# Cross-attention pair on one core: pair loop written out, row of maxima ahead of the loads of K and V, and eight slots in four batches with a second VectorE sum in the second attention

## The reference

```python
def layer0(Q, K, V):                      # 8 heads of 16; Q = x, K = V = ctx
    Qh, Kh, Vh = heads(Q @ W_q), heads(K @ W_k), heads(V @ W_v)
    attn = softmax(Qh @ Kh.T / sqrt(16))
    X = Q + merge(attn @ Vh) @ W_o
    return relu(X @ w1.T + b1) @ w2.T + b2 + X

def layer1(q_x, kv_x):                    # 16 heads of 32; q_x = layer0's result, kv_x = ctx
    q  = heads(layernorm(q_x) @ Wq.T)
    k, v = heads(layernorm(kv_x) @ Wkv.T)
    attn = softmax(q @ k.T / sqrt(32))
    x = q_x + merge(attn @ v) @ Wo.T + bo
    return x + silu(x @ W1.T + b1) @ W2.T + b2
```

## Time and profile before

| | |
|---|---|
| time, median of 3 runs (lowest, highest) | 5593.9 us (5593.8, 5606.19) |
| the profiled execution: its time, its span | 5599.11 us, 5597.3 us |
| granted TensorE clock, mean | 0.973 |
| TensorE (PE) busy | 5326.1 us, 95% |
| VectorE (DVE) | 4013.6 us, 72% |
| ScalarE (ACT) | 3170.5 us, 57% |
| GpSimd (POOL) | 2330.6 us, 42% |
| DMA, mean over the span | 58 GB/s |

### The profile page before, as it was taken

The page is one execution under the profiler, slowest core; times in us unless marked ns, Lnnn a source line. Parts: engine busy times, 40 slices in busy tenths (PEclk is TensorE's granted clock), DMA queues, the critical chain, the costliest instruction groups (busy, mean ns, idle before and its releaser), DMA issues. The chain is left out here.

```text
span 5597.3 us, 103454 instructions
## 1 busy us (share of the span) xinstructions
PE 5326.1 (95%) x28684; PEld 3349.3 (60%) x28684; DVE 4013.6 (72%) x6947; ACT 3170.5 (57%) x5792; POOL 2330.6 (42%) x1156
## 2 busy tenths in 40 slices
PE   8989999999799799999999999999999996999999
PEld 6744444444377456555565556555565563777777
DVE  6688888899577688887887878888788885332331
ACT  4257777788533366666666666666666664322222
POOL 0000000000000388888888878878888886000000
PEclk9989999999899799999999999999999998999999
DMA  7521111111343311111111111111111112322220
GB/s 214 128 47 38 36 36 39 36 38 32 98 134 108 102 41 28 40 40 41 39 29 41 40 41 34 36 39 40 41 29 40 41 28 63 111 93 68 86 88 23
DMA packets 329713, 325.64 MB, mean 58 GB/s; under 512 B 185744, under 2 KB 193808, under 8 KB 327184
## 3 DMA queue, kind: packets, MB, share of 16 engines
q1 hardware_dynamic: 329232, 319.92, 21.7%
HBM read 219.18 MB, written 100.53 MB: 57 GB/s over the span
## 5 line engine op out<-in xcount | busy, mean ns | idle before, releaser
L428 DVE TENSOR_REDUCE a_maxes<-a_mscore 128x1 f32<-128x458 f32 (+4 forms) x5376 | 3040.1, 625 | 652.6 <-PE a_mscore L487 625.2
L411 ACT ACTIVATE a_prob<-a_score 128x512 f32<-128x512 f32 x4992 | 2633.7, 599 | 1252.0 <-PE a_score L496 1222.8
L496 PE MATMUL a_score<-a_q,a_k 97*128 97x512 f32 (+1 forms) x4992 | 1987.3, 432 | 60.1 <-DMA a_q<-row 37.4
L487 PE MATMUL a_mscore<-a_k,a_qm 96*128 96x458 f32 (+4 forms) x5376 | 1896.7, 416 | 53.7 <-DMA a_k<-k 52.5
L515 PE MATMUL a_acc<-a_prob,a_v 128*32 128x512 f32 x9984 | 1604.0, 605 | 0.0
L487 PEld LDWEIGHTS a_mscore<-a_k,a_qm 96*128 96x128 f32 (+1 forms) x5376 | 1478.9, 310 | 174.9 <-issue 54.1
L377 POOL TENSOR_TENSOR a_added<-a_added,a_prob 128x1024 f32<-128x1024 f32 x640 | 1530.2, 2391 | 55.8 <-POOL a_added L377 0.6
L496 PEld LDWEIGHTS a_score<-a_q,a_k 97*128 97x128 f32 (+1 forms) x4992 | 921.3, 194 | 1026.7 <-ACT a_prob L411 532.7
L374 POOL TENSOR_TENSOR a_added<-a_prob 128x1024 f32<-128x1024 f32 x128 | 305.2, 2384 | 1924.6 <-ACT a_prob L411 1914.2
L510 PE MATMUL a_acc<-a_prob,a_ones 128*1 128x512 f32 x2048 | 965.2, 594 | 0.0
L515 PEld LDWEIGHTS a_acc<-a_prob,a_v 128*32 128x32 f32 x9984 | 292.6, 109 | 298.8 <-issue 152.3
(11 more groups left out here) (205 smaller groups left out, 3867.6 us busy)
## 6 DMA issues: line engine op xcount, KB each, us to landing
a_qm<-q SPq DMA_DIRECT2D x384, 64.0 KB, 1.9
a_q<-q SPq DMA_DIRECT2D x384, 64.0 KB, 1.9
acc<-a_acc_sb SPq DMA_DIRECT2D x384, 64.0 KB
e_part<-acc SPq DMA_DIRECT2D x90, 256.0 KB, 3.5
a_k<-k SPq DMA_DIRECT2D x48, 416.0 KB, 5.8
q<-m_qout SPq DMA_DIRECT2D x128, 128.0 KB, 2.3
e_wo<-wo_split SPq DMA_DIRECT2D x32, 512.0 KB, 4.2
k<-kv_k1out SPq DMA_DIRECT2D x24, 512.0 KB, 2.9
```

Source lines behind the costliest of these rows:

```text
L411: act.activation(prob[:, t], score[SCORES[it.j][t]][:], ACT.Exp, scale=SCALE).then_inc(exp_done, 1)
L428: dve.tensor_reduce(maxes[j][:, t, c:c + 1], mscore[u % UNIT_BANKS][:, 0:wide], AX.X, ALU.max).then_inc(unit_read, 1)
L487: pe.matmul(mscore[u % UNIT_BANKS][:, 0:wide], qm[j][r:r + ROW, t:NB:NB // P], kt[kk][r:r + ROW, at:at + wide], start=True, stop=True).the ...
L496: pe.matmul(score[SCORES[it.j][t]][:], kt[it.k][r:r + C, i * P:(i + 1) * P], qt[it.j][r:r + C, :], start=True, stop=True).then_inc(score_d ...
```

## The change

- **Loops:** the pair loop of `items` is gone: all pairs are written out. The inner loop over items stays.
- **SP:** in the first item of a head the row is moved first, then K and V are loaded. This holds in both attentions.
- **Second attention, slots:** slots 0 and 1 weigh four tiles each (0 to 7), slots 2 to 7 three each. Column group 3 so carries values in slots 0 and 1, and in slots 2 to 7 the sums of tiles 8, 11, 14, 17, of tile 25 ("rest") and `total`. Four batches of two slots, behind tiles 16 and 22 of the item and 7 and 12 of the next.
- **Side:** the values of group 3 are copied by ScalarE behind tile 19 (`copy_side`) into a tile `side`, stored by SP as a fourth accumulator array; the second batch waits for the copy. The copy of `acc` moves from tile 10 to tile 14.
- **VectorE:** a second `vsum`, over tiles 0 to 3 (512 elements an output quarter instead of 384), at tiles 9, 12, 15 and 19 of the item; that over 22 to 24 now at tiles 0, 3, 4 and 7 of the next. GpSimd's six wide additions take tiles 4 to 7, 9 and 10, 12 and 13, 15 and 16, 18 and 19, and 20 and 21, and it then adds the first `vsum`, its two halves and the second `vsum`. A new table `more` moves the units.
- **`ending`:** four accumulator parts; where the reciprocals and sums are held changes to make room.

```diff
@@ Layout, second attention
-            self.ROWS, self.SIDE, self.SUMS = 128, 3, 1
-            self.slots = [[(0, 3 * i), (1, 3 * i + 1), (2, 3 * i + 2), (3, ("one", 3 * i))] for i in range(8)]
-            self.slots.append([(0, 24), (1, 25), (3, ("sum", None))])
-            self.batches = [[0, 1], [2, 3], [4, 5], [6, 7], [8]]
-            self.at = {3: (3, True), 9: (4, True), 14: (0, False), 19: (1, False), 25: (2, False)}
-            self.copy_at = 5
+            self.ROWS, self.SIDE, self.SUMS = 128, 4, 1
+            self.slots = [[(c, 4 * i + c) for c in range(4)] for i in range(2)]
+            for i in range(2, 8):
+                first = 8 + 3 * (i - 2)
+                what = ("one", first) if i < 6 else ("rest", ST - 1) if i == 6 else ("sum", None)
+                self.slots.append([(0, first), (1, first + 1), (2, first + 2), (3, what)])
+            self.batches = [[0, 1], [2, 3], [4, 5], [6, 7]]
+            self.at = {7: (2, True), 12: (3, True), 16: (0, False), 22: (1, False)}
+            self.copy_at, self.side_at = 14, 20
+            self.first_at, self.later_at = (9, 12, 15, 19), (0, 3, 4, 7)
@@ items
-            yield from pair(0, True, False)
-            with eng.Fori(1, PAIRS - 1) as p:
-                yield from pair(p, False, False)
-            yield from pair(PAIRS - 1, False, True)
+            for p in range(PAIRS):
+                yield from pair(p, p == 0, p == PAIRS - 1)
@@ SP
+                if APART:
+                    sp.wait_ge(side_copied, n + 1)
+                    sp.dma_start(acc_out[ATEND, bass.ds(h * hd, hd), cols], side[3 * 32:P, :]).then_inc(side_stored, 16)
...
-                if it.starts_head and not it.first and not it.final_head:
-                    load_kv(it.h + 1, 1 - it.k)
                 if not it.last:
                     move_row(it.n + 1, 1 - it.j, it.next_use)
+                if it.starts_head and not it.first and not it.final_head:
+                    load_kv(it.h + 1, 1 - it.k)
@@ GpSimd
-                for i in range(1, 7):
-                    pool.wait_ge(exp_done, it.n * ST + 3 * i + 3)
+                for i, t in enumerate((6, 9, 12, 15, 18, 20)):
+                    pool.wait_ge(exp_done, it.n * ST + t + 2)
...
-                pool.tensor_tensor(added[0:LAST_KEYS, 1], added[0:LAST_KEYS, 1], prob[0:LAST_KEYS, 25],
-                                   ALU.add).then_inc(add_done, 1)
+                pool.tensor_tensor(added[:, 0], added[:, 0], vsum[:, 0], ALU.add).then_inc(add_done, 1)
@@ ScalarE
+            def copy_side(n):
+                act.wait_ge(pv_done, n * NBATCH + 1)
+                act.wait_ge(side_stored, n * 16)
+                act.activation(side[3 * 32:P, :], acc[3 * 32:P, :], ACT.Copy).then_inc(side_copied, 1)
@@ VectorE
+                    if APART and t in L.later_at and not it.first:
+                        add_up(it.n - 1, 1, L.later_at.index(t))
+                    if APART and t in L.first_at:
+                        add_up(it.n, 0, L.first_at.index(t))
@@ TensorE, weigh
+                if b == 1 and APART:
+                    pe.wait_ge(side_copied, n + 1)
@@ ending, normalise: SIDE is now 4
                 for s in range(1, SIDE):
                     dve.tensor_tensor(to[:, 0], to[:, 0], to[:, s], ALU.add).then_inc(sum_done, 1)
```

92 lines of the change are left out of this document (50 added, 42 removed).

## The result

| | before | changed |
|---|---|---|
| time, median (lowest, highest) | 5606.2 us (5593.8, 5609.2), 5 runs | 5642.3 us (5639.8, 5657.1), 5 runs |
| ratio | | 1.0075, 95% interval 1.0056 to 1.0095 |
| span of the profiled execution | 5597.3 us | 5640.4 us |
| first attention, 63 steps of the row of maxima | 1128.1 us | 1097.3 us |
| second attention, 127 steps of GpSimd's first addition | 2786.7 us | 2835.4 us |

The runs of before are those made beside the changed kernel, so its median differs a little from the one forecast against. The change costs 36 us by the medians and 43 by the spans, and the rows account for it: 127 x 0.61 = 77 more for the regular items, 29 less for what the second attention loses at its heads (2835.4 - 127 x 22.30 = 3, where it was 32), 31 less in the first attention, 25 more behind the last item: 77 - 29 - 31 + 25 = 42.

A forecast was written before the change was run, and what follows sets the result against it. TensorE's own work was taken as the bound, 20.65 us an item for 21.69. Items -132, heads -60 and ending +15 gave -177: 5422 us for the profiled execution, 5420 for the median, range 5350 to 5500.

The forecast's parts named there:

- The 20.18 us of TensorE's own work: Second attention, an item: 11.90 us of pairs and single products plus 8.28 of slots and batches, instead of 9.47.
- 8 x 0.88: Second attention, an item: eight slots at 0.88 us each, the price of a slot in the kernel before.
- Waits in the long run: TensorE's eleven tiles without a batch: scores wait some 0.4 us for ScalarE; 0.47 an item in all, bounds 0.1 and 1.1.
- a score needs the exponential three tiles back: Second attention: the reuse distance assumed when pacing TensorE's 0.44 us a pair against ScalarE's 0.52 us an exponential.
- VectorE's pieces: Second attention: four more sums over four tiles at 0.64 us each, VectorE's item 20.43 us, under TensorE's 20.65.
- Heads: Both attentions: moving the row of maxima and writing out the pair loop takes 60 us off, bounds 40 and 66.
- The rival by which the excess at the heads stays: Excess comes from K and V loads themselves and code fetched anew anyway, so it stays: 5480 us, chance 0.06.
- Ending: A fourth accumulator part to load and one more addition for each of 32 tiles: +15 us, bounds 3 and 35.
- The six waits: Ending: TensorE's six waits behind VectorE each get 1.9 us longer, 1.2 for the load and 0.7 for the addition.
- Side copy and store: Second attention: ScalarE's extra copy and SP's extra store cost nothing; 1.0 us an item is the far end.
- VectorE as a second bound: Second attention: VectorE, with only 0.2 us of slack, makes an item 21.2 us; 70 us more, 5490, chance 0.25.
- The slower one: Sharing memory with GpSimd stretches each four-tile piece from 0.64 to over 1.1 us; 5830 at 1.5 us each, chance 0.04.

The follow-up runs named there:

- experiment 5: A kernel of its own, TensorE slots with a sum over 128, 64, 32 or 2 partitions: 0.86 us a slot with 128, 1.91 to 1.94 with fewer.
- experiment 4: The changed kernel with VectorE's first sum over three tiles and tile 3 added by GpSimd, nothing left out: 5650.4 us, ratio 1.0089 to the kernel before.
- experiment 7: The changed kernel with tile 25 summed over 128 partitions, VectorE's first sum over three tiles, tile 3 on GpSimd: 5503.5 us, ratio 0.9829 to the kernel before.
- experiment 11: The kernel of experiment 7 with the batch at tile 7 moved to tile 4: 5571.5 us, ratio 0.9954 to the kernel before.
- experiment 12: The kernel of experiment 7 with score banks reordered, so tile 0 no longer takes the bank of two scores back: 5466.8 us, ratio 0.9747 to the kernel before.
- experiment 6: The changed kernel with tile 25 summed over all 128 partitions, by a column zero below the two real keys: 5585.4 us, ratio 0.9973 to the kernel before.
- experiment 8: The kernel before with the pair loop written out and the row of maxima moved ahead of K and V: 5531.2 us, ratio 0.9878.
- experiment 10: The changed kernel with the ending reading three accumulator parts of four: 5623.0 us, ratio 1.0045 to the kernel before.
- experiment 1: A kernel of its own, VectorE's sum in several shapes, GpSimd idle or adding: three tiles 0.50 us, four 0.93; four pieces 3.84 us beside GpSimd, 3.78 without.

## Why the prediction was wrong

**Slots and batches: the saving is there, one product was never priced.** The 20.18 us of TensorE's own work held to 0.1: three of the four batches and three of the four runs of tiles are as costed. The failed step is the term "8 x 0.88" for the eight slots: it gives the price of a slot of the kernel before to the slot with the sum of tile 25, which takes 1.94 us by itself (experiment 5). The prediction's one doubt at this place, whether "a slot with four weighing products costs no more than one with three and a sum", was about two other slots, and those came out as taken. The sum of tile 25, which GpSimd had added before, became a product over two partitions, and it costs 1.08 us an item, 137 us in all; experiments 4 and 7, which differ in nothing else, are 1.07 us an item apart. I priced products by columns and did not look at partitions. The kernel before has no such product, but the change names it.

**Waits in the long run: right in kind, too small by 0.5 us.** Forecast 0.4 there and 0.47 in all, measured 0.95; the bound of 1.1 held it. I had assumed that "a score needs the exponential three tiles back". At the border of two items it is two back. Experiments 7, 11 and 12 show a wait that starts there, depends little on the run's length (0.15 us for three tiles) and shrinks by 0.34 us when the border is mended. The 0.6 us that are left then are the part that the prediction had described, ScalarE's pace, for which it took 0.4.

**VectorE's pieces: mis-sized, 1.0 us for 0.64.** "By elements the wider sum is 0.50 to 0.67" was no bound; it was an assumption that the next tile costs what the third did. By the one element a cycle that the prediction quoted from the Trainium skill ("VectorE: DVE Perf Modes") the piece would be an estimated 0.53 us; the trace has 0.99, and the measurement decides. The advice of the Trainium skill against such a reduction on a hot path (same page, Rules for kernel authors) stands all the better. At 21.9 us an item VectorE was second behind TensorE, so the error cost nothing in this kernel and 82 us (experiment 7 against 6) in the one that mends TensorE alone.

**Heads: right.** -60 forecast; 31 + 29 = 60 in the changed kernel by the pitch of 21.69, 68 in experiment 8, which is over the bound of 66: the pitch of the earlier trace rows was a little high, and the loss at the heads with it 6 us too small. The rival by which the excess at the heads stays falls. The larger part, 45 us, is the row that waited behind the loads of K and V, 24 the written-out loop.

**Ending: +25 for +15**, inside its bounds. The six waits were taken at 11.4 us more, and TensorE waits 11.5 more, though in ten waits and not in longer six. What was not in the sum is 7 us more of busy time, of products that take a little longer in a stretch whose granted clock is slightly lower (experiment 10), and the start moved by 6 us instead of 4.

**Side copy and store: nothing, as taken.** By the list of waits TensorE's weight loads wait 29 us for the copy over 127 items, 0.23 each, and the run of tiles ahead of that batch shows no excess (8.02 us for the three runs, 7.98 by their prices). No wait for its store is among the larger ones.

**The sum.** Forecast 5422 for the profiled execution; add 127 x (22.30 - 20.65) = 210 for the item and 10 for the ending: 5642. Of the 1.65 us, 1.08 is the narrow product, 0.48 the waits and 0.1 the rest of TensorE's own work.

**The rivals.** The first, VectorE as a second bound, had the right engine at too small a price, and TensorE hid it. The slower one had four per cent and the wrong mechanism: pieces of 1 us were there, but not from shared memory, which adds under 2% (experiment 1), and not on the path. The chance of slower was too small for a plain reason: TensorE's item was counted in detail, and each kind of instruction that the change brings new (a product over two partitions, a reduction over four strided tiles) got the price of its nearest kin. Twice the kin's price would have been near for both: the piece takes 0.99 us and its kin 0.50, the slot 1.94 and its kin 0.86. With the slot at twice 0.88 alone the item has 20.65 + 0.88 = 21.5 us, 5530; with the piece at twice the 0.64 that was taken, VectorE's item is 17.87 + 4 x 1.28 = 23.0, and the range reaches beyond the result.

## What to carry to other kernels

Go through the diff for instruction forms that the old trace does not have, by partitions and strides as well as by size, and give each a bound of at least twice its kin; where TensorE packs columns, keep every product in the pack over the same 128 partitions, with zeros in the stationary column for what should not count. When two engines stand at nearly the same item time, taking one's load away shows nothing or too little: VectorE's gave 0, TensorE's 57, both 139 us. Bank and buffer orders have to be looked at over the border of two iterations, where the distance of reuse can be one less than inside.
